# A graph network layer stack on one core: the bias of the first messages moves to a product of one row, the copy out of the bank to ScalarE

## The reference, cut to what matters

```python
h = jnp.maximum(_layernorm(x, axis=-1), 0.0)
for l in range(3):
    def mlp(z):
        return jnp.maximum(z @ W1[l] + b1[l], 0.0) @ W2[l] + b2[l]
    msgs = mlp(h[col])                                     # col = dst
    agg = jax.ops.segment_sum(msgs, row, num_segments=N)   # row = src
    h = mlp(h + agg)
out = x + h @ Wf + bf
```

## Time and profile before

| What | us |
|---|---|
| median of three runs | 2256.65 (2256.49 to 2256.9) |
| the profiled execution, its own time | 2256.61 |
| its span in the profile | 2254.9 |
| maxima of the blocks (line 782), first and last start | 80.2 to 182.7 |

### The profile page before, as it was taken

One profiled execution on the slowest core, in us unless ns is written; L12 is line 12 of the kernel. 1 busy time (PEld: TensorE's weight loads), 2 busy tenths in 40 slices (PEclk: granted clock), 3 DMA queues, 4 the chain that ended last, 5 costly groups with the idle time before them and its releaser, 6 DMA issues.

```text
span 2254.9 us, 39446 instructions
## 1 busy us (share of the span) xinstructions
PE 2096.7 (93%) x15866; PEld 1153.6 (51%) x15866; DVE 1512.7 (67%) x1683; ACT 663.7 (29%) x1632; POOL 643.7 (29%) x287
## 2 busy tenths in 40 slices
PE   3566779999999999999997999999999999999998
PEld 3444445555555555545553555555555555555554
DVE  7899999999999999846645434444463443444344
ACT  4885655555555555411200000000010000000000
POOL 3666667777767776500000000000000000000000
PEclk8796999999999999999998999999999999999999
DMA  7256666666666666642343435444444554555552
GB/s 194 71 139 180 178 181 189 182 188 196 190 188 193 185 187 176 186 125 72 122 127 110 146 111 160 151 128 145 143 132 134 157 165 126 169 159 159 145 157 68
DMA packets 332824, 344.46 MB, mean 153 GB/s; under 512 B 21562, under 2 KB 303992, under 8 KB 332184
## 3 DMA queue, kind: packets, MB, share of 16 engines
q1 hardware_dynamic: 327516, 335.59, 50.6%
q0 software_dynamic: 2352, 6.43, 1.1%
q10 hardware_dynamic: 2816, 0.53, 0.2%
HBM read 252.58 MB, written 89.89 MB: 152 GB/s over the span
## 4 chain that ended last, share of the span: by engine, by line
PE 80%; DVE 13%; issue 4%; DMA 2%; SPq 0%; ACT 0%; POOL 0%; DVEq 0%; POOLq 0%
PE ps L1438 46%; PE ps L1336 18%; DVE arena L752 6%; PE ps L1331 5%; PE ps L1307 5%; PE ps L1400 2%; DVE arena L760 2%; PE ps L1392 2%; PE ps L1416 1%; DMA arena<-counts_dram 1%; DVE arena L791 1%; DVE arena L799 1%; DVE arena L725 1%; SPq L439 0%; DVE msg L778 0%
## 5 line engine op out<-in xcount | busy, mean ns | idle before, releaser
L1438 PE MATMUL ps<-arena,parts 128*128 128x448 fp8e4 x5488 | 1054.0, 353 | 11.9 <-DVE arena L882 11.9
L1438 PEld LDWEIGHTS ps<-arena,parts 128*128 128x128 f16 x5488 | 535.1, 98 | 531.4 <-issue 44.7
L627 POOL TENSOR_TENSOR arena<-arena,weight_now 128x416 int32<-128x416 int32 x196 | 540.8, 2759 | 274.0 <-DVE arena L752 273.3
L866 DVE TENSOR_SCALAR arena<-arena 128x3136 uint16<-128x3136 uint16 x196 | 191.5, 977 | 624.5 <-PE ps L1438 617.9
L1336 PE MATMUL ps<-arena,parts 128*128 128x448 fp8e4 x2744 | 554.9, 353 | 1.5 <-DVE parts L832 1.5
L752 DVE TENSOR_TENSOR arena<-row_iota,key_now 128x4096 f16<-128x4096 f16 x196 | 446.3, 2277 | 0.0
L1336 PEld LDWEIGHTS ps<-arena,parts 128*128 128x128 f16 x2744 | 267.1, 98 | 296.9 <-issue 83.1
L1132 ACT ACTIVATE arena<-ps 128x800 uint16<-128x800 f32 x392 | 332.3, 874 | 73.2 <-PE ps L1307 64.1
L1200 ACT ACTIVATE arena<-ps,b1s 128x448 f32<-128x448 f32 x42 | 26.6, 634 | 943.5 <-PE ps L1392 943.5
L1307 PE MATMUL ps<-arena 128*128 128x53 fp8e4 x6272 | 204.3, 189 | 79.8 <-DVE arena L752 41.2
L1307 PEld LDWEIGHTS ps<-arena 128*128 128x128 f16 x6272 | 187.7, 98 | 151.4 <-DVE arena L752 95.5
(11 more groups left out here) (127 smaller groups left out, 1146.9 us busy)
## 6 DMA issues: line engine op xcount, KB each, us to landing
arena<-counts_dram SPq DMA_DIRECT2D x294, 784.0 KB, 4.6
counts_dram<-arena SPq DMA_DIRECT2D x784, 100.0 KB, 2.2
h_dram<-parts SPq DMA_DIRECT2D x2, 1536.0 KB, 7.2
edges_dram<-arena SPq DMA_DIRECT2D x2, 1400.0 KB
arena<-in_x_dram SPq DMA_DIRECT2D x14, 192.0 KB
out_dram<-arena SPq DMA_DIRECT2D x14, 192.0 KB
arena<-in_dst_dram SPq DMA_DIRECT2D x1, 1400.0 KB
arena<-in_src_dram SPq DMA_DIRECT2D x1, 1400.0 KB
```

The lines of the kernel that those rows point to most:

```text
L627: nc.gpsimd.tensor_tensor(pairs, pairs, weight_now[:, h * HW:(h + 1) * HW].unsqueeze(2).to_broadcast([P, HW, WORDS // 2]), ALU.mult).then_ ...
L866: v.tensor_scalar(spread[:, c % WIDE, 0, :].bitcast(U16), packed, 0x0F0F, None, ALU.bitwise_and)
L1438: last = t.matmul(ps[:, b, 0:NB], parts[:, c * CK + k, :], spread[:, c % WIDE, b // 2, at:at + NB].bitcast(F8), start=start, stop=stop)
```

## The change

For each tile of a message block TensorE first multiplies a row of ones (one partition) by the bias row (one partition, the 64 values twice) into the bank, and then adds the product with W2 to it. ScalarE copies the bank to SBUF, in the even group 2m + 2, behind make_h0, keep_h0 and, in its program, at the place after keep_keys (which has no part in even groups). VectorE keeps the maximum alone, at its old place in the odd group 2m + 3, and waits there for ScalarE's copy.

```diff
@@ VectorE
-            def keep_message(m):
-                n = min(MB, HALF_T - m * MB)
-                dve.wait_ge(s["message0_done"], m + 1)
-                to = halves[:, m * MB:m * MB + n, :, :]
-                v.tensor_tensor(to, ps[:, 2, 0:n * P].rearrange("p (k w d) -> p k w d", w=2, d=D),
-                                b2row[:, 0:1, :].unsqueeze(1).to_broadcast([P, n, 2, D]), ALU.add).then_inc(
-                    s["message_kept"], 1)
+            def find_message_peak(m):
                 dve.wait_ge(s["message_kept"], m + 1)
-                v.tensor_reduce(peak[:, m:m + 1], to, AX.XYZ, ALU.max, apply_absolute_value=True).then_inc(
-                    s["peak_found"], 1)
+                v.tensor_reduce(peak[:, m:m + 1], halves[:, m * MB:min(m * MB + MB, HALF_T), :, :], AX.XYZ, ALU.max,
+                                apply_absolute_value=True).then_inc(s["peak_found"], 1)
...
                 if k >= 3 and k % 2 == 1 and k // 2 - 1 < BLOCKS:
-                    keep_message(k // 2 - 1)
+                    find_message_peak(k // 2 - 1)
@@ ScalarE
+            def keep_message(m):
+                n = min(MB, HALF_T - m * MB)
+                act.wait_ge(s["message0_done"], m + 1)
+                a.copy(halves[:, m * MB:m * MB + n, :, :],
+                       ps[:, 2, 0:n * P].rearrange("p (k w d) -> p k w d", w=2, d=D)).then_inc(s["message_kept"], 1)
...
                 if h in (1, 3) and j < BUILD - 1:
                     keep_keys(j + 1, h // 2)
+                if k % 2 == 0 and 1 <= k // 2 <= BLOCKS:
+                    keep_message(k // 2 - 1)
@@ TensorE
                 for c in range(min(MB, HALF_T - m * MB)):
-                    last = t.matmul(ps[:, 2, c * P:(c + 1) * P], uS[:, c * P:(c + 1) * P], W2b[:, 0, :], start=True, stop=True)
+                    to = ps[:, 2, c * P:(c + 1) * P]
+                    t.matmul(to, ones[0:1, :], b2row[0:1, 0:1, :].to_broadcast([1, 2, D]), start=True, stop=False)
+                    last = t.matmul(to, uS[:, c * P:(c + 1) * P], W2b[:, 0, :], start=False, stop=True)
```

## The result

| | before | after |
|---|---|---|
| median of five runs, us | 2256.65 | 2297.45 (2293.92 to 2297.99) |
| ratio, 95% interval | | 1.0180 (1.0166 to 1.0194) |
| span of the profiled execution, us | 2254.9 | 2294.6 |
| first comparison (line 752) to last maximum, us | 119.1 | 158.9 |
| mean granted clock of TensorE in the span | 0.976 | 0.96 |

The change makes the kernel slower by 1.8%, some 41 us. The forecast was 18.7 us and its range ended at 2281. It arises in the stage of the messages: the stage from VectorE's first comparison to its last maximum is 39.7 us longer, and so is the span (2294.6 - 2254.9). What comes later takes as long as before to within 1.5 us (the last reloaded counts are unpacked at 973.6 us, before at 932.5).

A forecast was written before the change was run, and what follows sets the result against it. VectorE sets the pace in the message stage, ScalarE close behind. Block delays 1.6 + 15.2 - 0.2 + 1.2 + 1.2 - 0.3 = 18.7 us, added to 2256.65, gave 2275.3 us; range 2266 to 2281.

The forecast's parts named there:

- The mechanism and the sign: Message stage: ScalarE's copy behind make_h0 and keep_h0 makes VectorE's maximum wait, 18.7 us slower; chance of slower 0.89.
- its own terms: Delays, bias products free: block 0 +1.6, blocks 1-8 +15.2, block 9 -0.2, block 10 -0.1, block 11 -0.7, block 12 -0.3 us.
- half of the delay: Whole kernel: the case taken as the lower end of the forecast range, given as 2266 us.
- rival E: Stage after 350 us: full engines take up half of the delay, 2265 us; chance 0.05.
- the price of the bias product: TensorE, message blocks: between nothing and the message product's own cost; upper end taken, +1.2 us each in blocks 10 and 11.
- the longer product is hidden: TensorE, blocks 1 to 8: doubled products of block 3 end at 105.2, before ScalarE is free at 107.23.
- The upper bound: TensorE: a bias product costs at most a message product; four take 1.06 us in block 3, 1.92 in block 11.
- Rival D: TensorE, message stage: lower granted clock adds 0.3 to 0.8 us for each of ten blocks, 2278 to 2283; chance 0.10.
- Rival B: VectorE, message stage: finds the copy ready and simply loses the adds, 8.4 us, giving 2248.2; chance 0.05.
- Rival C: ScalarE, message stage: amount of work decides, 8.38 us in a pair of 8.40; no change, 2254 to 2260; chance 0.05.
- The prediction's other way to B: ScalarE's order: with the copy ahead of make_h0, VectorE would find it ready and lose only the adds, 2248.2 us.
- The bounds of the range: Whole kernel: 2266 to 2281 us over all cases, from half the delay to rival D.

The follow-up runs named there:

- e2: Kernel after without the bias product, ScalarE's copy and the maximum at their old places: 2274.14 us, ratio 1.0076.
- e1: Kernel after with the bias product of each tile taking 128 rows in place of one: 2275.25 us, ratio 1.0082.
- e5: Kernel after with one one-row bias product of 512 columns a block in place of one each tile: 2282.09 us, ratio 1.0096.
- e9: Kernel after with one bias product a block, 512 columns and 128 rows, maximum at its old place: 2273.99 us, ratio 1.0070.
- e10: Kernel after with one 128-row bias product a block and each maximum one pair of groups later: 2247.54 us, ratio 0.9957.
- e12: Kernel after without the bias product and with each maximum one pair of groups later: 2250.44 us, ratio 0.9968.
- e6: Kernel after with one one-row bias product a block and each maximum one pair of groups later: 2252.24 us, ratio 0.9974.

## Why the prediction was wrong

**The mechanism and the sign were right, for one half.** The copy stands behind make_h0, VectorE waits for it, and the delay comes back in every pair. e2 measures that part by itself: +16.3 us. The prediction gives 16.5 for it, but its own terms add up to 15.5 (1.6 + 15.2 - 0.2 - 0.1 - 0.7 - 0.3); both lie within the noise of the measurement. The details held in e2 too (in blocks 1 to 8 idle times of 2.4 to 2.7 us and pairs of 10.3 to 10.6). Another slip changes nothing: half of the delay gives 2266, where rival E says 2265.

**The step that failed** is the price of the bias product: "Below it costs nothing, above as much as the message product itself", and with it the sentence that in blocks 1 to 8 "the longer product is hidden", because doubled the products end at 105.2. The upper bound was no bound. I priced the added product alone, from the row of its neighbour, and took the neighbour's own price as given. What the rows show in its place is that the alternation of 1 and 128 rows makes both products slow: four tiles take 3.2 us at full clock where I had 2.1, and 5.65 at half clock where I allowed 3.8. With that, TensorE ends last in most pairs: 25.6 of the 50.0 us of VectorE's idle time. e1 makes the row counts equal and comes to 2275.25, 17.4 us above the kernel before on its chip, where the forecast was 2275.3 and 18.7: the forecast is about the time of this kernel with a bias product of 128 rows. That the two times agree to 0.1 us is luck.

**Rival D** (a lower granted clock) had a part and was priced too low, 2278 to 2283. The clock of the stage fell from 0.90 to 0.62 in the kernel after, and I had given it 0.3 to 0.8 us a block, as a cost beside the bias product. It multiplies that cost instead. At full clock the alternating products of 3.2 us end before ScalarE is free (blocks 4 and 8, pairs of 10.3 us). At half clock products of equal rows do so nearly always (e1: a block in 3.4 us, pairs of 10.3 to 10.6). With alternation and half clock together, 5.65 us, TensorE ends last in every one of these pairs; with the fewer changes of e5 and half clock, 3.87 us, it does so by less. The Trainium skill, "TensorE: Matmul & The Clock Gate", What's actually happening, says that how busy the engine has been sets the gate. The busy time of the profile doesn't tell which way the clock will go here: from 85 to 170 us it is larger in e5 (66.19 us) than in e9 (57.61), at the lower clock, and a product also takes longer at the lower clock.

**Rival B** (VectorE simply loses the adds, 2248.2) needed the copy to be ready when VectorE comes. It is what e10 builds, by letting VectorE come later rather than ScalarE earlier: 2247.54. **Rival C**, ScalarE's load as the limit, may have its place there as well (ScalarE is never idle from 85 to 150 us), but no run shows that it sets the pace. The prediction's other way to B, the copy ahead of make_h0 on ScalarE, was not tried. **Rival E** had none: no more than 1.5 us of the delay was taken up after the messages.

The bounds of the range were too narrow on the side where the price was unknown. None of the rows of before that I used shows products with different row counts in turn (the trace has a single one-row product, line 1364 at 188.29, one column wide and alone behind a group), and that was the thing to see: an operation that differs from its neighbours in shape can change their price.

## What to carry to other kernels

When a small operation is put between equal ones on a pipelined engine, price the sequence and not the addition: here a bias product of one row more than tripled the time of the tile at full clock (0.84 us against a quarter of 1.06). If a row has to be added by a product, give it as many rows as its neighbours (identity times the row on all partitions); made once for the bank (e9) or once a tile (e1) it costs the same within the noise. And when work moves to another engine, look where it lands in that engine's order and move the consumer to match: the same change is 1.8% slower with the maximum at its old place, and 0.17% faster with the maximum one step later, 0.43% with the right bias product.

## What the hardware showed that was not expected

- Products whose stationary operand has 128 rows, alternating with ones of 1 or 64 rows (f32, 128 columns each): 0.83 to 0.84 us a tile of two at full clock and 1.45 at half. With equal rows 0.47 and 0.85. The weight loads of the alternating ones begin only near the end of the product before. The Trainium skill, "TensorE: Matmul & The Clock Gate", The mechanism, says that loads overlap with running products only where the row groups differ, and in the same section that a load into the background weight buffer is pulled ahead too. Here loads of equal, full row groups begin ahead of their products (the kernel before, e1), as the second sentence allows and the first does not, and those of a full group in turn with a partial one don't; the measurement decides.
- The number of rows in one product of 512 columns a block moves the granted clock of the stage from 0.66 (one row) to 0.82 (128 rows), with the same columns and number of products (e5, e9). With the maxima one pair later, where the pairs are of nearly the same length, the clock is 0.84 without a bias product (e12), 0.86 with one row (e6) and 0.94 with 128 rows (e10), and over the whole span 0.973 to 0.977, 0.972 to 0.977 and 0.978 to 0.979 in all executions. So there the product of 128 rows raises the clock, and the one of one row leaves it where it is without any. Why isn't shown.
